# Capacity layers of a twelve-layer macaron block: one-hots, ranks, output banks, and the order of features and routers at the barriers

## The reference

```python
m1 = one_hot(argmax(raw)); gate1 = sum(raw * m1)
m2 = one_hot(argmax(raw * (1 - m1))); gate2 = sum(raw * (1 - m1) * m2)
p1 = cumsum(m1) - m1
m1 = m1 * (p1 < C)
m1_count = sum(m1, over tokens)
p2 = cumsum(m2) - m2 + m1_count
m2 = m2 * (p2 < C)
combine = gate1 * one_hot(idx1) x one_hot(p1, C) + gate2 * one_hot(idx2) x one_hot(p2, C)
dispatch = combine != 0
hidden = gelu(dispatched @ w0) * (dispatched @ w1)
out = combined(hidden @ wo)
x = x + 0.5 * out      # the next layer starts with a layernorm of x
```

## Time and profile before

| what | us |
|---|---|
| median of three runs | 1765.02 (1763.72 to 1772.39) |
| the profiled execution | 1762.92 |
| its span in the trace | 1761.0 |
| lead-in of layer 0 | 0 to 25 |
| layer 0, and the way into layer 1 | 25 to 188 |
| layer 1 | 188 to 442 |
| layer 2 | 442 to 610 |
| layers 3 to 5 | 610 to 915 |
| layers 6 and 7 | 915 to 1105 |
| layer 8 | 1105 to 1236 |
| layer 9 | 1236 to 1367 |
| layer 10 | 1367 to 1632 |
| layer 11 | 1632 to 1761 |

### The profile page before, as it was taken

One profiled execution on the slowest core, in us unless ns is written; L12 is line 12 of the kernel. 1 busy time (PEld: TensorE's weight loads), 2 busy tenths in 40 slices (PEclk: granted clock), 3 DMA queues, 4 the chain that ended last, 5 costly groups with the idle time before them and its releaser, 6 DMA issues. The chain is left out here.

```text
span 1761.0 us, 25128 instructions
## 1 busy us (share of the span) xinstructions
PE 1517.7 (86%) x8766; PEld 1042.4 (59%) x8766; DVE 1230.0 (70%) x2815; ACT 1022.9 (58%) x1826; POOL 610.4 (35%) x738
## 2 busy tenths in 40 slices
PE   5999799998799799849999977997696799997696
PEld 4777323333577588637888965897696422222695
DVE  6687778994778744473535967596786778884785
ACT  3553478887554455345537732774374488887374
POOL 2675311121387200023006733673423211111423
PEclk9999989999899899969999988898798899999898
DMA  3121634400221400010000000000564633300564
GB/s 115 50 73 32 119 45 55 55 1 1 82 73 41 140 23 1 0 40 9 1 1 12 1 1 1 1 1 1 156 188 139 161 64 55 54 1 1 158 197 146
DMA packets 100757, 101.05 MB, mean 57 GB/s; under 512 B 23344, under 2 KB 86360, under 8 KB 99769
## 3 DMA queue, kind: packets, MB, share of 16 engines
q1 hardware_dynamic: 97687, 93.39, 21.7%
q0 software_dynamic: 2944, 6.05, 1.0%
HBM read 87.60 MB, written 15.78 MB: 59 GB/s over the span
## 5 line engine op out<-in xcount | busy, mean ns | idle before, releaser
L2636 DVE TENSOR_REDUCE mx<-bank 128x1 f32<-128x512 f32 (+1 forms) x512 | 320.2, 680 | 60.1 <-PE bank L2427 59.2
L2573 ACT ACTIVATE e<-bank 128x512 f32<-128x512 f32 x512 | 273.1, 599 | 53.6 <-PE bank L2459 50.7
L2459 PE MATMUL bank<-qq,kk 99*128 99x512 bf16 (+1 forms) x512 | 166.3, 391 | 13.4 <-ACT e L2573 12.8
L1565 POOL TENSOR_TENSOR midl<-mid,midh 128x512 fp32r<-128x512 f32 (+1 forms) x96 | 137.3, 1442 | 67.7 <-ACT midh L1485 67.4
L2459 PEld LDWEIGHTS bank<-qq,kk 99*128 99x128 bf16 (+1 forms) x512 | 39.3, 98 | 163.8 <-ACT e L2573 121.3
L1068 DVE TENSOR_TENSOR hl<-q,hh 128x512 fp32r<-128x512 f32 x64 | 44.8, 700 | 125.6 <-ACT hh L1038 103.7
L96 PE MATMUL bank<-wdh,midh 128*128 128x256 f32 (+1 forms) x384 | 113.8, 296 | 10.1 <-DVE x L1549 9.7
L227 POOL TENSOR_SCALAR rs<-mv 128x4 f32<-128x4 f32 x48 | 12.7, 265 | 288.4 <-DVE mv L214 287.5
L98 PE MATMUL bank<-wdh,midl 128*128 128x256 f32 (+1 forms) x384 | 110.9, 289 | 0.0
L97 PE MATMUL bank<-wdl,midh 128*128 128x256 f32 (+1 forms) x384 | 110.7, 288 | 0.0
L1480 ACT ACTIVATE mid<-bank,bu 128x512 f32<-128x512 f32 (+1 forms) x96 | 65.9, 687 | 64.8 <-PE bank L98 60.2
(11 more groups left out here) (406 smaller groups left out, 4429.2 us busy)
## 6 DMA issues: line engine op xcount, KB each, us to landing
w<-in_L_ffn_W SPq DMA_DIRECT2D x30, 512.0 KB
w<-in_L_ffn_W SPq DMA_DIRECT2D x30, 256.0 KB
qq<-scratch SPq DMA_DIRECT2D x18, 384.0 KB
w<-in_L_ffn_w_kernel SPq DMA_DIRECT2D x16, 344.0 KB
w<-in_L_ffn_w_kernel SPq DMA_DIRECT2D x16, 320.0 KB
wo<-in_L_ffn_wo_kernel SPq DMA_DIRECT2D x16, 320.0 KB
scratch<-e SPq DMA_DIRECT2D x34, 128.0 KB, 4.3
sorted<-in_unsorted SPq DMA_DIRECT2D x2, 1935.0 KB, 11.0
```

Source lines behind the costliest of these rows:

```text
L1565: e.tensor_tensor(l[0:fn, o], mid[i % 2][0:fn, o], h[0:fn, o].bitcast(F32), ALU.subtract).then_inc(*l2_m_lo.tick(n, i, f))
L2459: e.matmul(b_bank(t, u, j), keys(kk[0:K], t, b)[:, k * 128:(k + 1) * 128], queries(qq[0:K], t, b), start=True, stop=True).then_inc(*at_b.t ...
L2573: e.activation(er[u][:, j * 512:(j + 1) * 512], b_bank(t, u, j), ACT.Exp, bias=0.0, scale=scale).then_inc(*at_e.tick(n, t, u, j))
L2636: e.tensor_reduce(mxa[t % 3][:, o:o + nkb], bank[place_a["a", t, u, j]].rearrange("p (k n) -> p k n", k=nkb), X, ALU.max).then_inc(*at_max ...
```

## The change

Ranks: the masks `< 64` and the count's minimum are gone. A position over 64 matches no column of the one-hot anyway, and a group's full count puts the second choice over 64 as the capped one does. The count is added on TensorE, in the same accumulation as the second rank. One-hots: expert 0's low parts are made by VectorE behind the one-hots, and not by GpSimd; the up-projections of expert 0 wait for `w_set`. End: all four chunks of output have a bank pair each, the third and fourth those of the last up-projection and of the turns; the transpositions take the banks of chunk 0, the query the bank of chunk 1. Lead-ins: `halve_dve` of a settled stage or of a layer normalised by ScalarE comes behind the last `norm_dve`; with `paired` (the start and the stage of layer 7) TensorE transposes a chunk ahead of the router of the chunk before it. Ahead of layer 1 the third part comes behind the features, and each part is stored as soon as it is there.

```diff
@@ -300,12 +300,6 @@
                 stats_dve(q, m, c)
                 if c == 3:
                     pre.dve(q)
-                    if settled:
-                        pre.halve_dve(q, 1)
-                        pre.halve_dve(q, 2)
-                    elif scalar_norm(m, 2):
-                        pre.halve_dve(q, 0)
-                        pre.halve_dve(q, 1)
                 if c > 0 and not (c == 3 and settled):
                     norm_dve(q, m, c - 1)
...
@@ -327,16 +321,29 @@
...
-            for c in range(CHUNKS):
-                if c == 2:
-                    pre.closing_pe(q)
-                if c == 3 or c == 2 and not stage.settled:
+
+            def made(c):
+                if c == 3 or not stage.settled:
                     features_pe(q, m, c, stage)
+
+            def route(c):
                 if pre.route is not None:
                     q.wait_ge(*xt_set.at(m, c))
                     for t in range(4 * c, 4 * c + 4):
...
+                    return a
+
+            route(0)
+            if not stage.paired:
+                route(1)
+            pre.closing_pe(q)
+            made(2)
+            route(1 if stage.paired else 2)
+            made(3)
+            if stage.paired:
+                route(2)
+            a = route(3)
             if pre.route is not None:
                 a.then_inc(*route_mm.tick(m))
...
+            pre.ending_act(q)
 
         def begin_dve(q, m, stage, pre):
             norm_dve(q, m, 3)
-            for c in range(3 if stage.settled else 2 if scalar_norm(m, 2) else 0, CHUNKS):
+            for c in range(1 if stage.settled else 0, CHUNKS):
                 pre.halve_dve(q, c)
...
-                e.matmul(bank[4][:, 0:64], onesb, m4(m1b)[:, :, 0, :], start=True, stop=False)
-                e.matmul(bank[4][:, 0:64], onesb, m4(m1b)[:, :, 1, :], start=False, stop=True).then_inc(*rank.tick(n, "count"))
                 q.wait_ge(*mask_set.at(n, 2))
-                e.matmul(bank[5][:, 0:128], tri, m2b, start=True, stop=False, skip_group_check=True)
+                for j in range(2):
+                    e.matmul(bank[5][:, 0:128], onesb, m4(m1b)[:, :, j, :].unsqueeze(2).to_broadcast([128, 8, 2, 8]), start=(j == 0),
+                             stop=False, skip_group_check=True)
+                e.matmul(bank[5][:, 0:128], tri, m2b, start=False, stop=False, skip_group_check=True)
                 e.matmul(m4(bank[5][:, 0:128])[:, :, 1, :], onesb, m4(m2b)[:, :, 0, :], start=False, stop=True,
                          skip_group_check=True).then_inc(*rank.tick(n, 2))
...
-                    q.wait_ge(*w_lo.at(n, i, 1))
+                    q.wait_ge(*(w_lo if i > 0 else w_set).at(n, i, 1))
...
-                    w = wide[c % 2]
+                    w = wide[c]
...
                 eo_turn(3, 1, bank[6])
-                for c in range(2):
+                q.wait_ge(*mul_set.at(n, 7, 5))
+                combine(2, 0, 3)
+                for c in range(3):
                     combine(c, 3, 4).then_inc(*y_done.tick(n, c))
+                q.wait_ge(*gates_set.at(n, 3, 1))
+                combine(3, 0, 4).then_inc(*y_done.tick(n, 3))
                 for c in range(CHUNKS):
-                    if c >= 2:
-                        q.wait_ge(*xsum.at(m, c - 2))
-                        combine(c, 0, 4).then_inc(*y_done.tick(n, c))
                     finish_pe(q, m, c, stage, nxt)
...
                 q.wait_ge(*rank.at(n, 1))
-                chain(e.scalar_tensor_tensor(tmp, t3(bank[3]), 64.0, m1, ALU.is_lt, ALU.mult))
-                chain(e.scalar_tensor_tensor(q1, t3(bank[3]), 1.0, tmp, ALU.add, ALU.mult))
-                q.wait_ge(*rank.at(n, "count"))
-                chain(e.tensor_scalar(cnt, bank[4][:, 0:64].rearrange("p (g e) -> p g e", e=8), 64.0, None, ALU.min))
+                e.scalar_tensor_tensor(q1, t3(bank[3]), 1.0, m1, ALU.add, ALU.mult).then_inc(*step.tick())
                 q.wait_ge(*rank.at(n, 2))
-                chain(e.tensor_tensor(rest.rearrange("p (g j) e -> p g j e", j=2), m4(bank[5][:, 0:128]),
-                                      cnt.unsqueeze(2).to_broadcast([128, 8, 2, 8]), ALU.add))
-                chain(e.scalar_tensor_tensor(tmp, rest, 64.0, m2, ALU.is_lt, ALU.mult))
-                chain(e.scalar_tensor_tensor(tmp, rest, 1.0, tmp, ALU.add, ALU.mult))
+                chain(e.scalar_tensor_tensor(tmp, t3(bank[5]), 1.0, m2, ALU.add, ALU.mult))
...
                 for t in range(NT):
                     one(t)
+                for k in range(2):
+                    w, low_w = w_in[0][k]
+                    q.wait_ge(*w_hi.at(n, 0, k))
+                    e.tensor_tensor(low_w, w, wh[0][k].bitcast(F32), ALU.subtract).then_inc(*w_set.tick(n, 0, k))
...
                 e.memset(G[:, :, 8:32], 0.0).then_inc(*w_lo.tick(n, "pad"))
-                split_in(0, 0)
-                split_in(0, 1)
...
             def free(q, what):
-                if what == "logits":
-                    q.wait_ge(*gates_set.at(n, 3, 1))
-                else:
-                    q.wait_ge(*(mul_set.at(n, 7, 5) if what < 2 else xt_set.at(m, what - 2)))
-
-            stage = Stage(pe, act, dve, pool, sp, {0: 4, 1: 5, 2: 4, 3: 5, "logits": 6}, free)
+                q.wait_ge(*(xsum.at(m, 0) if what < 2 else xt_set.at(m, what - 2)))
+
+            stage = Stage(pe, act, dve, pool, sp, {0: 0, 1: 1, 2: 0, 3: 1}, free)
...
-            stage = Stage(pe, act, dve, pool, sp, {0: 6, 1: 7, 2: 6, 3: 7, "logits": 5}, free)
+            stage = Stage(pe, act, dve, pool, sp, {0: 6, 1: 7, 2: 6, 3: 7, "logits": 5}, free, paired=True)
...
-                q.e.matmul(bank[7], wq, XT[m % 2][:, 0:512], start=True, stop=True).then_inc(*qk_mm.tick(m, 0))
+                q.wait_ge(*xsum.at(m, 1))
+                q.e.matmul(bank[3], wq, XT[m % 2][:, 0:512], start=True, stop=True).then_inc(*qk_mm.tick(m, 0))
 
             def act(q):
                 q.wait_ge(*qk_mm.at(m, 0))
-                q.e.activation(full, bank[7], ACT.Identity, bias=bcol, scale=1.0).then_inc(*qk_full.tick(m, 0))
+                q.e.activation(full, bank[3], ACT.Identity, bias=bcol, scale=1.0).then_inc(*qk_full.tick(m, 0))
                 q.wait_ge(*qk_rem.at(m, 0))
                 q.e.copy(parts[1], rem).then_inc(*qk_second.tick(m, 0))
+
+            def ending_act(q):
                 q.wait_ge(*qk_rest.at(m, 0))
                 q.e.copy(parts[2], rem).then_inc(*qk_third.tick(m, 0))
...
+
+            def closing_dve(q):
                 q.wait_ge(*qk_second.at(m, 0))
-                e.tensor_tensor(rem, rem, parts[1], ALU.subtract).then_inc(*qk_rest.tick(m, 0))
-
-            def late(q):
-                q.wait_ge(*qk_third.at(m, 0))
-                for j in range(3):
+                q.e.tensor_tensor(rem, rem, parts[1], ALU.subtract).then_inc(*qk_rest.tick(m, 0))
+
+            def issue(q):
+                for j, ready in enumerate((qk_first, qk_second, qk_third)):
+                    q.wait_ge(*ready.at(m, 0))
                     store_runs(q, 0, j, parts[j], scr_in[0].land(m))
-
-            def issue(q):
                 q.wait_ge(*scr_in[0].at(m))
...
-        start = Stage(None, None, None, None, None, {0: 4, 1: 5, 2: 6, 3: 7, "logits": 0}, lambda q, what: None)
+        start = Stage(None, None, None, None, None, {0: 4, 1: 5, 2: 6, 3: 7, "logits": 0}, lambda q, what: None, paired=True)
```

14 lines of the change are left out of this document (7 added, 7 removed).

## The result

The changed kernel takes 1752.87 us (median of 5 runs, 1749.72 to 1754.43) against 1768.27 us of the kernel before beside it (1763.72 to 1772.39). The ratio is 0.9915, 95% interval 0.9892 to 0.9939: 15 us less, with an interval from 11 to 19. Forecast were 1753.9, and faster by over 0.5% with a chance of 0.75. The forecast fall was 11.1 us, at the small end of that interval; it was taken off 1765.0, the median known then, and not off 1768.27. The profiled execution took 1751.81 us (span 1750.0), where the sum of steps had given 1751.8. That this agrees to a hundredth is luck: two traces of the changed kernel further down differ by 7.2 us. Most single places scatter far less, so the steps are compared there.

A forecast was written before the change was run, and what follows sets the result against it. No single busiest engine: twelve layers with barriers, each bound by the engine holding the barrier. -2.0 - 6.7 + 0 + 0.75 - 2.1 - 1.4 + 0.35 = -11.1 us; forecast median 1753.9 us, range 1749.5 to 1760.

The forecast's parts named there:

- Ranks: Start of layers 0 and 2: three VectorE operations instead of seven ahead of the one-hots, -1.0 us each, -2.0 in all.
- One-hots: Layers 0 and 2: one-hots without GpSimd beside them, first up-projection 11.5 us behind the first; -3.7 and -3.0, together -6.7 us.
- the branch over TensorE and ScalarE: Dispatch of layers 0 and 2: three matmuls, last cast and handovers behind the last one-hot, ready at 11.5 us.
- the catching up: Dispatch matmuls start cold; they end as early as VectorE allows if the clock rises within 6.0 us; about five taken.
- The subtractions: Expert 0's two subtractions on VectorE behind the one-hots: 1.6 us, ready at 11.3, hidden by the dispatch.
- Four bank pairs: End of layers 0 and 2: TensorE has all chunks ready, but chunk 3's wait is off the path; 0 us.
- Third store: Ahead of layer 1: third query part made later, its store issued 0.6 us later, loads delayed; +0.75 us, bounds 0 and +2.9.
- Halves: Ahead of layers 2, 9 and 11 -0.6 us each, layer 6 -0.3: subtractions moved out of GpSimd's 1/sigma; -2.1 in all.
- Features ahead of routers: Lead-ins of layers 0 and 8: two 0.68 us waits for copies vanish in layer 0, -1.4 us, up to -2.4.
- Layer 8: Lead-in: the same two waits go, but chunk 1's router moves to the half clock; +0.35 us, or -0.7 if clock stays up.
- Expert loop: Loop of a capacity layer, TensorE busy 116.1 of 120 us at the full clock; the change leaves it alone.

The follow-up runs named there:

- before_split: Kernel before with only expert 0's two subtractions moved from GpSimd to VectorE behind the one-hots; 0.9954 of the kernel before.
- pool_split: Changed kernel with expert 0's weight subtractions back on GpSimd while VectorE writes the one-hots; 1758.87 us, 0.9973 of the kernel before.
- masks_back: Changed kernel with the ranks computed as before, by seven VectorE operations and separate counting matmuls; 1769.23 us, beside 1781.8 for the kernel before.
- the repeat: Changed kernel run once more without an edit, beside the second run with the query's third part made early; 1751.23 us, 0.9920 of the kernel before.
- the unpaired kernel: Changed kernel with layer 8's lead-in in the old order, each later router right behind its own transposition; 1765.0 us, beside 1781.8 for the kernel before.
- the combined kernel: Changed kernel with the query's third part early, twelve extra matmuls around the dispatch and 69 more from layer 2's end; 1753.07 us, 0.9924 of before.

## Why the prediction was right, point by point

- **Ranks** (-1.0 in each of two layers): 0.94 and 0.95, right.
- **One-hots** (-3.7 and -3.0): 3.31 and 2.63. The mechanism was right and no one-hot is long, but the branch over TensorE and ScalarE is ready at 11.9, not 11.5. The term that was mis-sized is the catching up: the clock rose after about 5 us as I took it, and the last product ended 10.8 us behind the first one-hot as my sum says. But I asked only whether TensorE catches up. ScalarE's casts, twelve in a row for 6.16 us, were still behind by the cold first groups; for 11.5 the clock has to rise within 4.1 us, not 6.0. The subtractions (1.68 us, forecast 1.6) stay hidden. Undone alone, the part costs 4.0 and 3.0 us.
- **Four bank pairs** (0): 0 in the profiled pair and in layer 2. I took the idle time and the length of chunk 3's products from one trace, in which the clock happened to be high; in `before_split`, at the low clock, the old form paid 1.5 us, through the query's product behind them on TensorE, a path that I had not followed.
- **Third store** (+0.75): 0.0 at the loads. The step that failed is the last copy's time. I let the last transpositions take 1.11 us as before; they ran at the full clock, 0.66, so the third store went out 0.14 us later, not 0.6, and landed 1.9 us behind its issue. In `pool_split` and `masks_back` they start at the same distance and do take 1.11: there the third store went out 0.6 us later, as forecast, and the loads 0.45. So against the kernel before the term is 0.0 or 0.45, by a clock that I had fixed at one value; what sets it there is open. The 1.3 us that the scores are late are a time from loads to scores that scatters. My own first explanation of them fell in the repeat.
- **Halves** (-2.1): 3 x 0.64 + 0.34 = 2.26, right.
- **Features ahead of routers**, layer 0 (-1.4, to -2.4): from first statistics to logits 17.60 before and 15.50 in every changed trace, -2.1, without any rise of the clock. Layer 8 (+0.35): -0.48 in the profiled pair, the wrong sign. One step failed in both: I counted a wait as the 0.68 us that the row shows ahead of the router. From a transposition's start to the router behind it it is 1.77 us with the wait and 0.89 without, and the router itself took 1.87 with it and 1.72 without: 1.03 us for each wait. Two of them are 2.1 in layer 0; in layer 8 the moved router takes 1.72 of it back, which leaves a gain of 0.34, and the unpaired kernel shows 0.31.
- **Expert loop** (untouched): 124.77 us instead of 124.33. A cast of GpSimd and a subtraction of VectorE meet; before, GpSimd's pair took 1.80 us and VectorE's operation 0.69, after, 1.21 and 1.12. Twelve traces show 124.75 to 124.81, the combined kernel and the one before 124.4 and 124.3. The forecast had nothing for it. The moved subtractions alone are not the cause, since `pool_split` without them has 124.76; what shifts the two operations onto each other is open.

The forecast sum came out because its errors had both signs: the one-hots brought 0.8 us less than forecast, the loops and the late scores cost 1.4 more, the two lead-ins with features ahead of routers and the halves brought 1.7 more than forecast, and work that the change leaves alone did the rest. The changed places of the profiled pair sum to -2.1 - 0.9 - 3.3 + 0.4 + 1.3 - 0.9 - 2.6 + 0.4 - 2.3 - 0.5 = -10.5 us (lead-in, ranks, one-hots, loop of layer 0, landing of the loads, ranks, one-hots, loop of layer 2, halves, layer 8). The rest of the -11.0 in the spans are +0.3 at start-up and -0.8 in work that the change leaves alone, itself the sum of steps between +1.5 and -2.4. The medians differ by 15.4 and, in the repeat, by 14.1 us (1765.31 and 1751.23). Where the further 3 to 4 us are is open; the one trace of the kernel before is of an execution of 1762.92 us, below all five of its runs beside the changed kernel, so no trace shows them. That the old end of layer 0 pays its 1.5 us in some executions of the kernel before would be a part; it is shown for another kernel only.

## What to carry over

Ask of a slow VectorE operation what GpSimd does at that moment, and move GpSimd's work behind it: here each GpSimd operation held up one VectorE operation, and one-operand work was no way out. Where TensorE waits for a copy, put independent matmuls there; the gain is the wait and the slower restart behind it. Read one place in several traces before explaining a microsecond: here most intervals that an edit sets repeat within 0.02 us, some take one of two values by the clock (18.45 or 18.91 us), and a landing or stretches of low clock move a layer by 1 to 5 us.

## What the runs showed of the hardware

GpSimd copies with one operand hold up VectorE's one-hots as well, 0.68 us each becoming 1.09, one one-hot for each copy. The Trainium skill (GPSIMD Engine Reference, Key points) names VectorE's instructions with two SBUF inputs as those that contend; the one-hots are such, and this trace agrees, with the share lost depending on GpSimd's operation (43% and 71%). My forecast said that VectorE stands still while GpSimd's operation with two operands runs; by these shares it does not do so for all of the time that the row gives that operation. The other surprise is how often the granted clock differs between two executions of one program in the same layer: low for 3.4 to 13.7 us in one stretch near the start of layer 1, a layer that took 243.3 to 248.8 us from the scores to the next logits.
